# A 64-row down product over all 128 rows, and a row gather issued ahead of a scatter's wait, in the expert stage of a decoder layer

## What is computed

```python
probs = jax.nn.softmax(logits, axis=-1)
topv, topi = jax.lax.top_k(probs, TOP_K)
gate_w = jnp.sum(jax.nn.one_hot(topi, E, dtype=flat.dtype) * topv[..., None], axis=1)
g = jnp.einsum('td,eid->tei', flat, w1)
u = jnp.einsum('td,eid->tei', flat, w3)
yexp = jnp.einsum('tei,edi->ted', jax.nn.silu(g) * u, w2)
moe_out = jnp.einsum('ted,te->td', yexp, gate_w).reshape(Bb, L, D)
```

## Time and profile before

| | us |
|---|---|
| median of 3 runs (lowest, highest) | 643.4 (642.71, 646.73) |
| the profiled execution | 645.63 |
| its span, first to last instruction | 643.9 |
| PE busy in the span | 594.2 (92%) |
| expert stage, first rows gathered to last result copied | about 260 to 453 |

### The profile page before, as it was taken

One profiled execution on the slowest core, in us unless ns is written; L12 is line 12 of the kernel. 1 busy time (PEld: TensorE's weight loads), 2 busy tenths in 40 slices (PEclk: granted clock), 3 DMA queues, 4 the chain that ended last, 5 costly groups with the idle time before them and its releaser, 6 DMA issues.

```text
span 643.9 us, 10884 instructions
## 1 busy us (share of the span) xinstructions
PE 594.2 (92%) x3641; PEld 447.2 (69%) x3641; DVE 464.9 (72%) x785; ACT 386.9 (60%) x880; POOL 298.7 (46%) x240
## 2 busy tenths in 40 slices
PE   4999779998999999999999999999999999998874
PEld 2653679887998887597778678779855555565541
DVE  6889899999999947534453542562565698999885
ACT  4589899999999956522241222221646665777443
POOL 6023599999999991223223234243113233134201
PEclk9999799999999999999999999999999999999898
DMA  8001551111121108424441432411610000000001
GB/s 281 3 1 37 161 216 66 51 60 56 50 66 50 35 19 317 164 86 160 168 170 31 169 124 77 138 63 30 214 65 1 1 1 1 1 1 1 2 0 66
DMA packets 18261, 51.50 MB, mean 80 GB/s; under 512 B 3842, under 2 KB 9603, under 8 KB 16548
## 3 DMA queue, kind: packets, MB, share of 16 engines
q1 hardware_dynamic: 15172, 41.43, 18.1%
q0 software_dynamic: 2752, 7.34, 4.0%
q10 hardware_dynamic: 288, 2.10, 0.9%
HBM read 46.21 MB, written 4.66 MB: 79 GB/s over the span
## 4 chain that ended last, share of the span: by engine, by line
PE 63%; ACT 13%; DVE 9%; DMA 8%; issue 5%; POOL 0%; POOLq 0%; DVEq 0%; ACTq 0%
PE ps L2156 9%; PE ps L2229 8%; ACT arena L661 7%; PE ps L2164 6%; DMA moe_out<-arena,result_now 5%; PE ps L2218 4%; PE ps L2250 3%; ACT arena L676 3%; PE ps L1939 3%; PE ps L1924 3%; PE ps L1970 2%; PE ps L1774 2%; PE ps L1765 2%; PE ps L2179 2%; DMA arena<-hn_rows,row_now 2%
## 5 line engine op out<-in xcount | busy, mean ns | idle before, releaser
L449 POOL TENSOR_TENSOR arena<-arena 128x1024 f32<-128x1024 f32 x64 | 149.5, 2370 | 4.5 <-DVE arena L1294 4.3
L1294 DVE TENSOR_TENSOR_SCAN arena<-arena,ps 128x1024 f32<-128x1024 f32 x64 | 143.4, 2279 | 5.1 <-remote 2.4
L661 ACT ACTIVATE arena<-arena,a_neg 128x510 f32<-128x510 f32 x128 | 84.7, 710 | 1.9 <-DVE arena L1294 1.9
L2156 PEld LDWEIGHTS ps<-arena 128*128 128x128 f32 x660 | 75.5, 192 | 3.5 <-issue 3.1
L2156 PE MATMUL ps<-arena 128*128 128x128 f32 x660 | 77.1, 276 | 0.0
L1924 PE MATMUL ps<-ident,arena 128*128 128x128 f32 x384 | 65.2, 280 | 9.9 <-ACT arena L672 7.6
L871 ACT ACTIVATE arena<-ps 128x256 f32<-128x256 f32 x45 | 17.3, 384 | 89.7 <-PE ps L2156 85.5
L1939 PE MATMUL ps<-ident,arena 128*128 128x128 f32 x512 | 67.1, 273 | 2.2 <-DVE arena L1303 1.8
L676 ACT ACTIVATE arena<-arena,b_tok 128x512 f32<-128x512 f32 x96 | 64.9, 710 | 0.0
L1939 PEld LDWEIGHTS ps<-ident,arena 128*128 128x128 f32 x512 | 57.8, 141 | 3.4 <-DVE arena L1303 1.3
L2229 PE MATMUL ps<-arena 128*128 128x512 f32 x128 | 58.2, 595 | 0.0
(11 more groups left out here) (312 smaller groups left out, 1168.2 us busy)
## 6 DMA issues: line engine op xcount, KB each, us to landing
arena<-in_w_moe SPq DMA_DIRECT2D x8, 2176.0 KB, 9.2
arena<-c_dram SPq DMA_DIRECT2D x32, 256.0 KB, 3.1
arena<-in_w_o ACTq DMA_DIRECT2D x1, 2048.0 KB, 14.6
arena<-in_w_qT SPq DMA_DIRECT2D x1, 2048.0 KB
arena<-moe_out SPq DMA_DIRECT2D x8, 256.0 KB, 4.9
arena<-in_w_q SPq DMA_DIRECT2D x1, 2048.0 KB
x<-in_x SPq DMA_DIRECT2D x2, 512.0 KB, 4.7
arena<-in_w_in SPq DMA_DIRECT2D x2, 512.0 KB, 5.8
```

The costliest lines, as they stand in the source:

```text
L449: pool.tensor_tensor(in_chunks(hC[unit % 3]), in_chunks(h[unit % 3]), c_bc[:, m % C_BUFS, :].unsqueeze(1).to_broadcast([P, 2, HALF]), ALU. ...
L661: ins = nc.scalar.activation(dA_b[:, unit % 2, 2 * k:2 * k + 2, 1:], dt_b[:, c, 2 * half:2 * half + 2, 1:], ACT.Exp, scale=a_neg[:, c, n:n ...
L1294: nc.vector.tensor_tensor_scan(h[unit % 3], dA[:, k, :], ps[:, 2 * k:2 * k + 2, :].rearrange("p a b -> p (a b)"), 0.0, ALU.mult, ALU.add). ...
L2156: ins = nc.tensor.matmul(ps[:, bank, c * P:(c + 1) * P], w13[:, k, chunk * P:(chunk + 1) * P], xT[:, k, :], start=(k == 0), stop=(k == KD ...
```

## The change

It has four parts. (1) `tail_down` multiplies all six chunks over 128 rows. The lower 64 rows of the sixth chunk of `hid` then have to be zero, and the memset that was made once ahead of the experts is made in every `gate_tail`, as its first instruction on DVE. (2) `move_rows` is cut in three: `rows_ahead` (index and gather of rows j+2), `stored` (wait for the landing of the scatter of unit j-1, count `y_free`), `store_rows` (index, wait for `y_ready`, scatter). The wait for a scatter thus moves behind the next unit's gather. (3) `VW_AHEAD` goes from 6 to 5, and product 5 moves into the first tail. (4) The index counts follow.

```diff
-        VW_AHEAD = 6
-        VW_TURNS = {0: ((6,), (7,)), 1: ((8, 9), (10,)), 2: ((11, 12), (13, 14)), 3: ((15,), ())}
+        VW_AHEAD = 5
+        VW_TURNS = {0: ((5, 6), (7,)), 1: ((8, 9), (10,)), 2: ((11, 12), (13, 14)), 3: ((15,), ())}
...
-            def move_rows(j, rows):
-
-                pool.tensor_copy(result_now[:, :], result_of[:, bass.ds(j, 1)]).then_inc(s["index_set"], 1)
+            def rows_ahead(j):
                 pool.wait_ge(s["xT_psum"], j + 3)
                 pool.sem_inc(s["waited"], 1)
                 pool.tensor_copy(row_now[:, :], row_of[:, bass.ds(j + 2, 1)]).then_inc(s["index_set"], 1)
+                pool.wait_ge(s["index_set"], 2 * j + 1)
+                pool.sem_inc(s["waited"], 1)
+                gather_rows(row_now[:, 0:1])
+
+            def stored(j):
+                pool.wait_ge(s["y_stored"], j * 16)
+                pool.sem_inc(s["y_free"], 1)
+
+            def store_rows(j, rows):
+                pool.tensor_copy(result_now[:, :], result_of[:, bass.ds(j, 1)]).then_inc(s["index_set"], 1)
                 pool.wait_ge(s["index_set"], 2 * j + 2)
                 pool.sem_inc(s["waited"], 1)
-                gather_rows(row_now[:, 0:1])
                 pool.wait_ge(s["y_ready"], j + 2)
                 pool.sem_inc(s["waited"], 1)
                 pool.indirect_dma_start(moe_out[:, :], bass.IndirectOffsetOnAxis(result_now[0:rows, 0:1], 0), y_row[0:rows, :], None).then_inc(s["y_stored"], 16)
-                pool.wait_ge(s["y_stored"], j * 16 + 16)
-                pool.sem_inc(s["y_free"], 1)
 
             last = 0
             for e in range(E):
-                move_rows(last, TAIL)
+                rows_ahead(last)
+                if e:
+                    stored(last)
+                store_rows(last, TAIL)
...
                 with pool.Fori(first + 1, last) as j:
-                    move_rows(j, P)
+                    rows_ahead(j)
+                    stored(j)
+                    store_rows(j, P)
...
             for n in range(VW_AHEAD):
-                take_values_times_output(n, (4, 5, 2, 3, 4, 5)[n])
+                take_values_times_output(n, (4, 5, 2, 3, 4)[n])
...
                 dve.wait_ge(s["gu_psum"], first * (FCH // 2) + FCH // 2)
+                nc.vector.memset(act_g3[TAIL:P, 2, P + REST:2 * P], 0.0)
...
             nc.vector.memset(hid[REST:P, WHOLE, :], 0.0)
-            nc.vector.memset(act_g3[TAIL:P, 2, P + REST:2 * P], 0.0)
...
                     for rows, chunk in ((0, c), (TAIL, FCH // 2 + c)):
-                        used = REST if chunk == WHOLE else P
-                        ins = nc.tensor.matmul(ps[rows:rows + TAIL, 6, 0:D], hid[0:used, c, rows:rows + TAIL], w2[0:used, chunk, :],
+                        ins = nc.tensor.matmul(ps[rows:rows + TAIL, 6, 0:D], hid[:, c, rows:rows + TAIL], w2[:, chunk, :],
```

## The result

| | before | changed |
|---|---|---|
| median of 4 runs each, us (lowest, highest) | 643.93 (642.71, 646.73) | 636.98 (635.17, 638.98) |
| ratio, 95% interval | | 0.9887 [0.9842, 0.9931] |
| the profiled execution, us (its span) | 645.63 (643.9) | 637.12 (635.1) |

Faster by 1.1%, against a forecast of 635.9 us. Measured again later, on the chip of the second group of experiments, the same kernel took 636.14 against 643.95, ratio 0.9878 [0.9858, 0.9898].

The account below looks back on a forecast made before the run. The prediction took PE to bound the expert stage. Its terms, 4.3 + 3.7 - 0.3 - 0.2 = 7.5 us, off the median of 643.4 gave 635.9 us, range 633 to 640.5.

Parts of the forecast that it names:

- PE's row, not the chain's DMA: Expert stage: PE sets the pace, so an edit is worth what it takes from PE's row, not from the chain.
- The gather ahead: Gather issued before the wait for the scatter: all five PE waits for rows go, 4.3 us won, bounds 0 and 4.8.
- The pair: Tail's down product, sixth chunk over 128 rows: 0.53 us less per tail in seven tails, 3.7 us won.
- Product 5: Moved into the first tail: PE idles ahead of it, partly repaid by cover ahead of L2103; net 0.3 us lost.
- The memset: One per tail on DVE, most hidden; 0.1 us lost in the fifth and sixth tail, 0.2 us together.
- Late all the same: A gather issued into the weight load stays held up and the five waits stay: 640.2 us, chance 0.11.
- The last pair serial: Tail's down product: the widened last pair still runs one half after the other, 638.9 us, chance 0.10.
- row tiling: Tail's down product: the 64-row pair is the quick form, so widening loses 1.8 us: 641.4 us, chance 0.03.
- The gather slowing the scatter: Both queue during a weight load; the scatter lands x later and delays the next tile: 647.8 us, chance 0.05.
- It moves nothing: The gain is taken back at a later meeting not seen: 643.4 us, chance 0.04.
- Sum: Over the expert stage: 4.3 + 3.7 - 0.3 - 0.2 = 7.5 us won, reaching the end whole.

Follow-up runs that it names:

- no_pair: The changed kernel with the sixth chunk over 64 rows again and the memset once ahead of the experts; 639.61 us, ratio 0.993 to the kernel before.
- memset_once: The changed kernel with the memset made once ahead of the experts instead of in each tail; 635.73 us in one run.
- gather_only: The kernel before with only `move_rows` cut in three in the new order; 639.83 us, ratio 0.9946.
- product_back: The changed kernel with product 5 ahead of the first tail again, nothing else; 635.02 us in one run.
- all_three: The changed kernel with the memset once, product 5 ahead of the first tail, and the tails' own result buffer; 634.76 us, ratio 0.9848 to the kernel before.
- order_load: The changed kernel with the memset once, product 5 ahead of the first tail, and the weight load held until the last scatter's landing; 638.44 us, ratio 0.9941 to the kernel before.

## Why the prediction was right

**PE's row, not the chain's DMA: right.** The scatter's share of the chain fell by 12.7 points of 200 us, some 25 us, and the stage by 7.95. The forecast took its sum from PE's waits and lines, and came within 0.5 us of the stage.

**The gather ahead, 4.3: 4.82 measured alone.** All five waits went. The step said "by 300" for the second expert; it was 298.1, by the mechanism given (with the held-up scatter, or just behind). The surplus lies in two experts. The fourth won 1.87 where 1.61 was counted: the scatter landed in 7.5 us in that execution and its whole tile ran free, 4.90 us after 5.05. The eighth won 0.83 where 0.6 was counted: this kernel has no memset in the tail, and L2113 waited for DVE less than I took it to. The step's upper bound of 4.8 is not worked out in it (3.9 and five times 0.15 make 4.65), and the measured 4.82 lies just above it.

**The pair, 3.7: 3.66.** The step from 1.96 to 1.43 was 1.96 to 1.39, and 0.57 a tail instead of 0.53: the one change of form left costs 0.06, not 0.10. The fourth expert wins nothing, as said: it took 23.86 us in `no_pair` and 23.90 in `memset_once`; the other seven win 0.43 to 0.60. That the sum comes out so close is in part luck, since 0.57 in seven tails would be 4.0. The rule of row tiling for short contractions, which the prediction names from the Trainium skill, was rightly set aside: the 64-row form, alone between 128-row ones, cost 0.57 us more. The same page of the Trainium skill, TensorEngine Tiling (Array Packing), says under Tiling Modes, Key Properties, that changing the mode drains the engine; the trace agrees, by the idle 0.39 that went with the 64-row form.

**Product 5, 0.3 lost: 0.1 at most.** `gather_only` and `no_pair` differ in it alone: their stages are 185.18 and 185.28, and from the first transposes to the second tail both take 25.78. The hole ahead of the first tail is there as forecast, but the tail's L2105 starts 2.15 us behind the first transpose instead of 2.23:

```profile
263.12 1.08 PE L2031 MATMUL ps<-arena 128*64 128x256 f32 x8
264.90 2.47 PE L2105 MATMUL ps<-arena 128*64 128x384 f32 x15 [0.69 <-issue]
...
269.35 0.44 PE L2075 MATMUL ps<-ident,arena 128*128 128x128 f32 x2
269.62 0.49 PE L2113 MATMUL ps<-ident,arena 128*128 128x128 f32 x3
```

This is the step's error: it took the stretch up to the tail's start to be as long as before. In the five kernels with product 5 in the tail it is 2.03 to 2.19 us, in the eight others 2.22 to 2.24. The cover counted was right (L2113 no longer waits); from the tail's start to L2113 it is 4.72 us after 4.46, near the 0.3 counted, and the earlier start gives part or all of that back. The step also left out that the same cover hides the memset, which costs the first tail 0.16 without it (L2113 waits 0.60 in `product_back` and 0.44 in `all_three`).

**The memset, 0.2 lost: 0.43.** This is the mis-sized term among the losses. Each takes 0.112 us, as priced, but moves the next step by 0.16 in the fifth tail (0.41 - 0.25), and from start to start by 0.11 in the fourth, 0.17 in the sixth and 0.21 in the eighth. These make 0.65, of which the stage shows 0.43: without the memset PE came earlier to the first whole tiles of the fourth and fifth expert and waited there for the product behind `y_free` (5.64 and 5.06 us after 5.49 and 4.90). The step named the fifth and sixth at 0.1 each, and had the eighth's inside the gather's term.

```profile
L1431 DVE MEMSET arena<- x8: 112/112/112, 268.5 to 424.6; 64x64 f32 x8
```

**The rivals.** Late all the same: not here, but it is what happens when the load starts later (`order_load`), so the 0.11 was on a real mechanism. The last pair serial, and row tiling: ruled out by the one row of twelve loads. The gather slowing the scatter: the held-up scatters take 7.5 to 8.6 us, before 7.5 to 8.5, so x is about 0. It moves nothing: the time behind the stage is 190.33 us after 190.93, within the 189.0 to 191.0 of all profiles, so no later meeting takes the gain back.

**Sum.** From the kernel before over `gather_only`, `no_pair` and `memset_once` to the changed kernel it is one edit at each step, and the stage moves by 4.82 less, 0.10 more (product 5), 3.66 less and 0.43 more. That these make the stage's 7.95 is so by construction and proves no term; and it holds in this order of the edits, since the pair pays 3.66 with the gather in time and 1.87 without, which the prediction did not say. Against its 7.5, the gather's term was 0.5 too small, the memsets' 0.2 too small and product 5's 0.2 too large. That the last two cancel is luck.

## What to carry to other kernels

A saving on the engine that sets the pace is worth only what the next meeting leaves of it: before adding up edits, work out for each place by how much the data waited for is early, and count the edit that makes it early first. Where small transfers and a bulk load run beside each other, look in the trace whether the small ones land with the end of the bulk load, as they did here, and decide by it when to issue either. A short instruction put ahead of a chain that another engine waits for cost that engine, here, about the instruction's length or up to twice that at every such place, of which a later wait can take a part back.

## What the hardware showed that I had not expected

- A gather issued 0.85 us behind the start of a 2176 KB load took 8.0 us to land, one issued 5.7 us behind the start of such a load 3.8, the median of all is 3.1. Both landed within about 1 us of the load's end. The first packet of a small transfer issued at the load's start ran 4.3 to 5.2 us behind the issue, and 1.5 to 1.8 where no load ran.
- The issue of an indirect DMA on POOL, 0.99 us in the median, took 1.58 to 1.78 in some places beside long DVE work (1.64 at 294.23, beside a DVE instruction that runs 1.61 us from 293.38). It explains little of the late landing: without a load, a scatter whose issue took 1.58 us landed in 3.0 us.
- A memset of 0.112 us moved the engine that waited behind it by 0.11 to 0.21.
